# A layer norm's passes taken off VectorE in a Perceiver block's second loop

## The reference, cut to what matters

```python
def _layernorm(x, axis=-1, eps=1e-05):
    m = jnp.mean(x, axis=axis, keepdims=True)
    v = jnp.var(x, axis=axis, keepdims=True)
    return (x - m) / jnp.sqrt(v + eps)

# L0_ffn
h = jnp.einsum('btd,hd->bth', x, absmean(W_fc))
h = jax.nn.gelu(h, approximate=False)
h = layernorm(h, ln_w, ln_b)
return jnp.einsum('bth,dh->btd', h, absmean(W_proj))
# L1_xattn
q = input_q @ Wq + bq      # input_q is a layer norm of the stream
# L1_attn: products of a layer norm of the stream with W_q and W_down_kv
```

## Time and profile before

| | us |
|---|---|
| median of 3 runs | 2119.76 |
| lowest and highest | 2118.71, 2125.53 |
| the profiled execution | 2121.26 |
| its span | 2119.5 |
| busy TensorE, VectorE, ScalarE, GpSimd | 1807.9, 1567.3, 1476.0, 1224.7 |
| the second loop's prologue, first load to last VectorE pass | 1395.9 to 1417.6 |
| the second loop, to the end of the span | 1418.0 to 2119.5 |

### The profile page before, as it was taken

How to read it: one execution, slowest core, us unless ns; L and a number is a source line. 1 busy time by engine, 2 the same in 40 slices (tenths; PEclk the granted TensorE clock), 3 DMA queues, 4 the chain that set the end, 5 groups by cost and what they waited for, 6 DMA issues and landing times. The chain is left out here.

```text
span 2119.5 us, 41548 instructions
## 1 busy us (share of the span) xinstructions
PE 1807.9 (85%) x14355; PEld 1208.1 (57%) x14355; DVE 1567.3 (74%) x2913; ACT 1476.0 (70%) x3431; POOL 1224.7 (58%) x1332
## 2 busy tenths in 40 slices
PE   4999899899889889889889886437899999999974
PEld 2665556556556556556556543135677777777753
DVE  3348777777767767767867867744799999999974
ACT  2558877877877877877877876702567777777764
POOL 1435555555555654644655554414788888888861
PEclk8999999999999999999999998767999999999985
DMA  7422122122122122112212111010000000000000
GB/s 178 138 90 68 45 73 73 45 73 73 45 73 66 52 64 64 63 55 71 65 43 73 43 41 49 1 59 11 6 17 15 12 12 15 15 12 15 12 9 11
DMA packets 48370, 103.20 MB, mean 49 GB/s; under 512 B 6384, under 2 KB 25072, under 8 KB 43376
## 3 DMA queue, kind: packets, MB, share of 16 engines
q1 hardware_dynamic: 48240, 101.57, 15.3%
HBM read 93.03 MB, written 8.52 MB: 48 GB/s over the span
## 5 line engine op out<-in xcount | busy, mean ns | idle before, releaser
L862 POOL TENSOR_TENSOR kcube<-kcube,ksq 128x512 f32<-128x512 f32 x128 | 179.1, 1399 | 463.9 <-ACT ksq L719 463.9
L697 ACT ACTIVATE abuf<-delta,cols 128x496 f32<-128x496 f32 x512 | 338.8, 700 | 30.8 <-DVE gP L944 14.4
L872 POOL TENSOR_TENSOR yac<-yac,gP 128x1024 f32<-128x1024 f32 x128 | 302.2, 2361 | 11.5 <-ACT gP L706 10.4
L944 DVE TENSOR_TENSOR_SCAN gP<-abuf,ps_s 128x512 f32<-128x512 f32 x256 | 293.4, 1196 | 0.6 <-POOL yac L872 0.6
L524 PE MATMUL ps_kv<-kcube,cx 128*128 128x256 f32 x1024 | 246.9, 384 | 32.1 <-ACT Gs L745 28.9
L944 DVE TENSOR_TENSOR_SCAN gL<-abuf,ps_s 128x512 f32<-128x512 f32 x192 | 223.3, 1206 | 57.2 <-ACT abuf L697 57.2
L512 PE MATMUL ps_kv<-w_k,cT 128*128 128x256 f32 x1024 | 264.7, 403 | 0.0
L570 PE MATMUL ps_t<-gL,diag 128*128 128x512 f32 x384 | 195.1, 633 | 54.3 <-DVE gL L944 49.1
L524 PEld LDWEIGHTS ps_kv<-kcube,cx 128*128 128x128 f32 x1024 | 191.8, 192 | 78.5 <-issue 50.3
L512 PEld LDWEIGHTS ps_kv<-w_k,cT 128*128 128x128 f32 x1024 | 190.3, 196 | 52.2 <-issue 30.1
L583 PE MATMUL ps_kv<-hT,w_pT 128*128 128x512 f32 x384 | 187.1, 610 | 18.8 <-ACT delta L770 14.4
(11 more groups left out here) (312 smaller groups left out, 4112.4 us busy)
## 6 DMA issues: line engine op xcount, KB each, us to landing
cT<-in_h_ctxT SPq DMA_DIRECT2D x32, 1028.0 KB, 5.0
cx<-in_ctx SPq DMA_DIRECT2D x32, 1024.0 KB, 5.7
xT<-in_h_xT SPq DMA_DIRECT2D x8, 512.0 KB, 3.6
xcur<-in_x SPq DMA_DIRECT2D x32, 128.0 KB, 2.0
x_mid<-xb SPq DMA_DIRECT2D x16, 256.0 KB, 2.2
x_c<-x_mid SPq DMA_DIRECT2D x32, 128.0 KB, 2.0
out<-y SPq DMA_DIRECT2D x32, 128.0 KB, 1.7
kv_all<-vleft SPq DMA_DIRECT2D x8, 256.0 KB, 10.6
```

The lines of the kernel that those rows point to most:

```text
L697: act.activation(abuf[q % 2][:, i, :].rearrange("p (b t) -> p b t", t=T)[:, :, 1:T], delta[J % 2][:, :].rearrange("p (b t) -> p b t", t=T) ...
L862: pool.tensor_tensor(t[:, :, :], t[:, :, :], ksq[:, :, :], ALU.mult).then_inc(S["k3_ready"], 1)
L872: pool.tensor_tensor(yac[:, :, :], yac[:, :, :], pool_home(q)[:, :, :], ALU.add).then_inc(S["pacc_done"], 1)
L944: dve.tensor_tensor_scan(dst[:, i, :], abuf[q % 2][:, i, :], ps_u[:, :], 0.0, ALU.mult, ALU.add).then_inc(S["scan_done"], 1)
```

## The change

Three layer norms of the second loop lose their VectorE pass.

- `gn` is gone. TensorE turns `ga` itself; `pjT` has its mean over the 1024 inputs subtracted; the root `g_r` is applied where `x3` is made. `x3` waits for `g_r`, and the GpSimd instruction that writes `g_r` waits for the `x3` of the group before. GELU waits for the turn and the statistics of the group before.
- `hd` is gone. TensorE turns `x3` itself; `wq` is centred; the root `d_r` is applied in the first `kq` pass. `x3` waits for the turn of the group before, `d_r` for the first `kq` pass of the group before.
- `he` moves to ScalarE, as a copy of `x4` with the root as scale, behind `qfT` and ahead of `heT`; `aq` and `dn` are centred.
- `prologue2` gets the means: TensorE sums the columns by a matrix of ones (2 matmuls for `dn`, 4 for `wq` and `aq`, 8 for `pjT`), VectorE subtracts them in four passes at its end.

```diff
@@ prologue2: tensor
             last.then_inc(s_dn, 1)
+            pe.wait_ge(s_rawdn, 1)
+            for dc in range(DC):
+                last = pe.matmul(ps_qmean2[:, 0:64], v["ones"][:, :], W["dn"][:, dc, :], start=(dc == 0), stop=(dc == DC - 1))
+            last.then_inc(s_dnmean, 1)
...
             last.then_inc(s_crow, 1)
+            pe.wait_ge(s_in, 16 * len(loads))
+            for dc in range(DC):
+                last = pe.matmul(ps_qmean[:, 0:D], v["ones"][:, :], W["wq"][:, dc, :], start=(dc == 0), stop=(dc == DC - 1))
+            for dc in range(DC):
+                last = pe.matmul(ps_qmean[:, D:2 * D], v["ones"][:, :], W["aq"][:, dc, :], start=(dc == 0), stop=(dc == DC - 1))
+            last.then_inc(s_qmean, 1)
+            pe.wait_ge(s_raw, 1)
+            for f in range(FC):
+                last = pe.matmul(ps_means[:, 0:D], v["ones"][:, :], W["pjT"][:, f, :], start=(f == 0), stop=(f == FC - 1))
+            last.then_inc(s_mean, 1)
@@ prologue2: vector
             dve.tensor_scalar(W["bq"], W["bq"], K_EPS, None, ALU.add)
+            dve.wait_ge(s_dnmean, 1)
+            dve.scalar_tensor_tensor(out=W["dn"][:, :, :], in0=ps_qmean2[:, 0:64].unsqueeze(1).broadcast_to([P, DC, 64]),
+                                     scalar=-1.0 / D, in1=W["dn"][:, :, :], op0=ALU.mult, op1=ALU.add)
+            dve.wait_ge(s_qmean, 1)
+            for w, k in (("wq", 0), ("aq", 1)):
+                dve.scalar_tensor_tensor(out=W[w][:, :, :], in0=ps_qmean[:, k * D:(k + 1) * D].unsqueeze(1).broadcast_to([P, DC, D]),
+                                         scalar=-1.0 / D, in1=W[w][:, :, :], op0=ALU.mult, op1=ALU.add)
+            dve.wait_ge(s_mean, 1)
+            dve.scalar_tensor_tensor(out=W["pjT"][:, :, :], in0=ps_means[:, 0:D].unsqueeze(1).broadcast_to([P, FC, D]), scalar=-1.0 / HF,
+                                     in1=W["pjT"][:, :, :], op0=ALU.mult, op1=ALU.add)
@@ pe_body
-            after(pe, "c_gn", g)
+            after(pe, "c_gelu", g)
             for hh in range(2):
-                last = turn(ps_cf[:, hh, :], gn[:, hh * 512:(hh + 1) * 512], 4, ident[:, :])
+                last = turn(ps_cf[:, hh, :], ga[:, hh * 512:(hh + 1) * 512], 4, ident[:, :])
...
-            after(pe, "d_h", g)
+            after(pe, "x3", g)
             after(pe, "d_t", g - 1)
             after(pe, "d_z", g - 1)
-            turn(ps_d, hd[:, :], DC, ident[:, :]).then_inc(S["d_turn"], 1)
+            turn(ps_d, x3[:, :], DC, ident[:, :]).then_inc(S["d_turn"], 1)
@@ act_body
             after(act, "c_fc", g)
-            after(act, "c_gn", g - 1)
+            after(act, "c_gturn", g - 1)
+            after(act, "g_bs", g - 1)
...
             act.activation(qfT[:, :, :], halves(ps_d[:, 0:D]), ACT.Copy).then_inc(S["d_qfT"], 1)
         g = s[3]
         if g is not None:
+            after(act, "e_rstd", g)
+            after(act, "e_turn", g - 1)
+            act.activation(he[:, :], x4[:, :], ACT.Copy, scale=sm["e_r"][:, 0:1]).then_inc(S["e_h"], 1)
             after(act, "e_turn", g)
@@ pool_body
             after(pool, "e_eps", g)
+            after(pool, "e_h", g - 1)
             pool.tensor_tensor(sm["e_r"][:, :], sm["e_ve"][:, :], nhalf[:, 0:1], ALU.pow).then_inc(S["e_rstd"], 1)
...
             after(pool, "g_eps", g)
+            after(pool, "x3", g - 1)
             pool.tensor_tensor(sm["g_r"][:, :], sm["g_ve"][:, :], nhalf[:, 0:1], ALU.pow).then_inc(S["c_gr"], 1)
...
             after(pool, "d_eps", g)
+            after(pool, "d_kb", g - 1)
             pool.tensor_tensor(sm["d_r"][:, :], sm["d_ve"][:, :], nhalf[:, 0:1], ALU.pow).then_inc(S["d_rstd"], 1)
@@ dve_body
-            after(dve, "d_rstd", g)
-            dve.tensor_scalar(hd[:, :], x3[:, :], sm["d_mv"][:, 0:1], sm["d_r"][:, 0:1], ALU.subtract, ALU.mult).then_inc(S["d_h"], 1)
...
             after(dve, "d_q", g)
-            dve.tensor_tensor(kq[:, :], ps_d[:, 0:D], W["bq"], ALU.add).then_inc(S["d_kb"], 1)
+            after(dve, "d_rstd", g)
+            dve.scalar_tensor_tensor(out=kq[:, :], in0=ps_d[:, 0:D], scalar=sm["d_r"][:, 0:1], in1=W["bq"], op0=ALU.mult,
+                                     op1=ALU.add).then_inc(S["d_kb"], 1)
...
-            after(dve, "e_rstd", g)
-            dve.tensor_scalar(he[:, :], x4[:, :], sm["e_mv"][:, 0:1], sm["e_r"][:, 0:1], ALU.subtract, ALU.mult).then_inc(S["e_h"], 1)
...
-            after(dve, "d_h", g - 1)
-            dve.tensor_tensor(x3[:, :], x_p[:, :], ps_c1[:, 0:D], ALU.add).then_inc(S["x3"], 1)
+            after(dve, "d_turn", g - 1)
+            after(dve, "c_gr", g)
+            dve.scalar_tensor_tensor(out=x3[:, :], in0=ps_c1[:, 0:D], scalar=sm["g_r"][:, 0:1], in1=x_p[:, :], op0=ALU.mult,
+                                     op1=ALU.add).then_inc(S["x3"], 1)
...
-            after(dve, "c_gr", g)
-            dve.tensor_scalar(gn[:, :], ga[:, :], sm["g_mv"][:, 0:1], sm["g_r"][:, 0:1], ALU.subtract, ALU.mult).then_inc(S["c_gn"], 1)
```

## The result

The median of the changed kernel is 2200.65 us (2200.38 to 2201.31), that of the kernel before beside it 2120.68 us. The ratio is 1.0377, with an interval of 1.0359 to 1.0395: slower by 80 us. The forecast was 36.7 us slower, with a range up to 2184. The direction was right, the size was not. The span of the profiled execution is 2198.6 us at a mean granted clock of 0.921 (before 2119.5 at 0.943).

The account below looks back on a forecast made before the run. It took the 18.99 us step to be bound by a ring through TensorE, which waits only for `pT_s` and `hd`. Loop 22.6, ramp 4.5, drain 3.6 and stage before 6 added 36.7 us, giving 2156.5 us, range 2130 to 2184.

Parts of the forecast that it names:

- Step (1): Loop without `gn` and `hd`: TensorE's wait for `hd` goes, giving back 0.58 us a step.
- Step (2): `he` on ScalarE behind `qfT`: `e_av` starts 1.57 us later, `kq` 0.99 us later after the 0.58 given back.
- Step (3): Behind `kq` in the loop: root on first pass costs nothing, second pass may give back 0.05 us, 0.5 at most.
- rival C: GpSimd starts before VectorE at `kTm` in the loop: 0.9 us more a step, 2178 us; chance 0.08.
- Step (4): GpSimd's `g_r` waits for the previous group's `x3`: about 0.5 us later, covered in the loop, a cost in the ramp.
- Step (5): The other new waits, of `x3`, GELU and `d_r`: no price, bounds 0 and 0.05 us each.
- Step (6): Stage before the loop, with the added means and subtractions: 6 us more, bounds 4 and 7.5.
- Ramp and drain: Partly filled steps around the loop: ramp 4.5 us more (bounds 2 and 6), drain 3.6 (2 and 4.5).
- Rival D: TensorE's waiting in one longer piece lowers its clock: 4 us in one loop step of four, 24 us, 2180; chance 0.05.

Follow-up runs that it names:

- e1_he_back: The changed kernel with `he` made VectorE's pass again, in its old place; 2130.11 us, ratio 1.0044 to the kernel before.
- e6_he_only: The kernel before with the new `prologue2` and, in the loop, only `he` moved to ScalarE behind `qfT`; 2200.23 us, ratio 1.0383.
- e3_filler: The changed kernel with 16 turns of the identity added on TensorE ahead of `he`'s turn; 2143.73 us, ratio 1.0115 to the kernel before.

## Why the prediction was wrong, step by step

- **Step (1), the gain at `hd`, 0.58 us: wrong in the cause.** The row names `hd` as what ended the wait. But `hd` was late because VectorE's whole queue was late, by its wait for `f_r` (0.36 us) and by `fq` beside `blk` (0.51 instead of 0.34). With `hd` gone the turn waits for `t_d` of the same queue, 0.42 us (`e1_he_back`). The prediction names that wait for `t_d` and doesn't ask when `t_d` comes. VectorE's own groups had the answer, 0.36 us a step for `f_r`, and the prediction rests on TensorE's waits alone. That the 0.58 us still came back in the sum is luck: in `e6_he_only` `hd` is still a pass of VectorE, and TensorE's wait for it is gone as well.
- **Step (2), `he`'s place: right.** 0.50 us, straight behind `qfT`, a turn 0.05 us later, `e_av` behind the turn, a single wait of 2.2 us. `e_av` started 0.37 us after the turn's start, not 0.44. Since the 2.2 us of waiting swallow what the queue behind them had been late by, what remains of step (1) doesn't matter here, and the sum of the step at full clock is right to 0.2 us: 0.94 forecast, 0.75 measured (`e3_filler`). `e6_he_only` shows that this one edit makes the whole loss.
- **Step (3): right.** `kq` takes 0.48 instead of 0.42, its second pass 0.73 instead of 0.92; VectorE is first at `kTm`, and rival C did not happen.
- **Step (4), `g_r`'s wait: wrong where it shows.** In the changed kernel the cover holds, as said: `e6_he_only`, which doesn't have this wait, is as slow. With `he` in time the cover is gone and it costs 0.10 to 0.16 us a step (19.12 to 19.02, 19.15 to 18.99), not the 0.5 that I gave as its price uncovered.
- **Step (5), no price for the other waits: right** as far as a trace shows it; none of them is in any list of the loop.
- **Step (6): 4.5 us, forecast 6, inside its bounds.** `pjT`'s passes ran at 0.23 us each, not 0.30.
- **Ramp and drain.** At full clock they add next to nothing: 22.8 us (`e3_filler`) less 18 and 4.5. Forecast were 8.1; in the changed kernel 7.5 us are there (80 less 50 for the clock in the loop, 18 and 4.5), but `e3_filler` shows that they go with the clock.
- **Rival D was the failed step: the sum has no term for the clock.** I gave it 0.05, with 4 us in one step of four. It came in every step, at 1.5 or 3.0 us, 2.08 on average (21.82 - 19.74), 50 us over the 24 steps. The ground against it, that the loop stays 88% busy, is true (53.36 of 60 us are 89%) and says nothing: waits of 0.73 and 0.58 us apart leave the clock of the kernel before at 1.00, and 1.7 times as much in one piece doesn't. The evidence that I used, nine microseconds of the drain at 0.57 behind long waits, was of too coarse a kind to tell 2.2 us from 7. Nothing in the trace of before has a wait of 2 us in a busy loop; the honest chance for an unknown of this size was not 1 in 20, and its upper end not 24 us.

Without the clock the measured terms give 2120.98 + 18 + 4.5 = 2143.5, which is `e3_filler`'s 2143.73; the forecast of 2156.5 was 13 us above that, by the loop (22.6 for 18), the ramp and drain (8.1 for nearly nothing) and the stage before (6 for 4.5).

## What to carry to other kernels

Before an edit merges TensorE's small waits into one long one, price the clock as its own term, in every turn of the loop; a pass that moves to an engine with more room is judged by the moment its result is ready there. Before a pass is dropped because TensorE waits for it, ask what the engine itself waited for on the way: here moving one small instruction on a third engine gave 0.37 us a step, and dropping two passes on top of it 0.05. Read the waits of all the engines on the ring, not of the last one alone.

## What I had not expected of the hardware

- With one wait of TensorE of 2.2 us in a step of 21.8 us the higher clock is lost for a while in every step; with one of 1.3 us in about every other step; with two of 0.7 and 0.6 us, a few microseconds apart, in none of the loop. But a short longest wait is no surety: four of the versions with 0.7 us and at most 0.4 beside it lost it in one or three of the 24 steps, and what sets those steps apart stays open. In the changed kernel and the runs with filler the loss comes in pieces of about 1.5 us a step; in the single steps it was 0.7 to 1.2 us.
- This kernel could be made faster by giving TensorE useless work: 16 turns of the identity per step took 57 us off.
- A small pass of VectorE (`fq`, 0.34 us alone) takes 0.85 us when it starts 0.7 us before the end of GpSimd's `blk`, and a small root of GpSimd (0.55 us alone) takes 1.07 to 1.32 us beside VectorE's `gn` and `hq`; what runs beside them and when decides their length more than their size.
